# Which engine normalises the third tile of the next block's input: GpSimd or ScalarE

## The reference

```
n = layernorm(x)
s = sigmoid(silu(n @ s_w1.T + s_b1) @ s_w2.T + s_b2)
u = (n @ B_w.T + B_b) * s
h[t] = h[t-1] @ A.T + u[t]                       # a scan over 4096 steps, state of 128
x1 = x + (h @ C_w.T + C_b + n @ D_w.T + D_b) * sigmoid(n @ g_w.T + g_b)
m = layernorm(x1)
e = argmax(m @ gate_w.T)                         # one of 8 experts for each row
out = x1 + (m + m @ expert_w[e].T)
```

## Time and profile before

| what | value |
| --- | --- |
| median of three runs | 909.34 us (908.67 to 910.84) |
| the profiled execution | 911.03 us, span of the core 909.2 us |
| TensorE busy | 890.7 us, 98% |
| VectorE busy | 684.2 us, 75% |
| ScalarE busy | 635.5 us, 70% |
| GpSimd busy | 426.8 us, 47% |
| blocks | from 15.1 us to about 675 us |
| granted TensorE clock | 0.998 of full |

### The profile page before, as it was taken

One profiled execution on the slowest core, in us unless ns is written; L12 is line 12 of the kernel. 1 busy time (PEld: TensorE's weight loads), 2 busy tenths in 40 slices (PEclk: granted clock), 3 DMA queues, 4 the chain that ended last, 5 costly groups with the idle time before them and its releaser, 6 DMA issues. The chain is left out here.

```text
span 909.2 us, 15716 instructions
## 1 busy us (share of the span) xinstructions
PE 890.7 (98%) x4413; PEld 719.8 (79%) x4414; DVE 684.2 (75%) x1697; ACT 635.5 (70%) x880; POOL 426.8 (47%) x671
## 2 busy tenths in 40 slices
PE   8999999999999999999999999999999999999996
PEld 7778878787887878787787878787878887888884
DVE  6778888888887888888887888888686465555552
ACT  5568697978879687977879687978634445666661
POOL 1134537282735537282836546282624453433442
PEclk9999999999999999999999999999999999999999
DMA  9436495867758486867768495856989979998871
GB/s 319 131 93 148 93 213 140 200 144 193 157 155 209 101 213 137 201 145 189 148 169 206 95 221 128 202 145 161 293 285 401 370 239 252 216 226 220 196 184 49
DMA packets 231050, 172.37 MB, mean 190 GB/s; under 512 B 155701, under 2 KB 189237, under 8 KB 229952
## 3 DMA queue, kind: packets, MB, share of 16 engines
q1 hardware_dynamic: 220032, 137.71, 60.8%
q0 software_dynamic: 10800, 33.70, 11.3%
q10 hardware_dynamic: 144, 0.07, 0.0%
HBM read 81.63 MB, written 54.68 MB: 150 GB/s over the span
## 5 line engine op out<-in xcount | busy, mean ns | idle before, releaser
L1798 PE MATMUL y<-experts,x1T_hi 128*128 x568 | 180.5, 399 | 0.7 <-DVE x1T_lo L1422 0.7
L666 POOL DMA_INDIRECT out<-gate,ids x71 | 72.6, 1023 | 110.3 <-DVE gate L1441 69.0
L602 POOL TENSOR_SCALAR ln_var_eps<-ln_mean_var 128x4 f32<-128x4 f32 x16 | 3.7, 231 | 252.6 <-DVE ln_mean_var L1097 252.5
L1798 PEld LDWEIGHTS y<-experts,x1T_hi 128*128 128x128 f32 x568 | 103.2, 188 | 20.6 <-issue 0.9
L1798 PE MATMUL y<-experts,x1T_lo 128*128 x284 | 111.4, 392 | 0.0
L1476 PE MATMUL gates<-GwT_hi,xT_hi 128*128 128x512 f32 x256 | 105.0, 410 | 1.6
L592 POOL TENSOR_TENSOR y_biased<-y_biased,gate 128x256 f32<-128x256 f32 x120 | 94.1, 805 | 23.8 <-DVE y_biased L1087 23.6
L1476 PE MATMUL y<-DwT_hi,xT_hi 128*128 128x512 f32 x256 | 102.6, 401 | 0.0
L1441 DVE TENSOR_TENSOR gate<-y,raw_weights 128x512 f32<-128x512 f32 x71 | 49.1, 691 | 69.2 <-PE y L1798 65.1
L1478 PE MATMUL gates<-GwT_hi,xT_lo 128*128 128x512 f32 x256 | 100.6, 393 | 0.0
L1477 PE MATMUL gates<-GwT_lo,xT_hi 128*128 128x512 f32 x256 | 100.6, 393 | 0.0
(11 more groups left out here) (285 smaller groups left out, 2335.1 us busy)
## 6 DMA issues: line engine op xcount, KB each, us to landing
raw_weights<-routed_rows SPq DMA_DIRECT2D x71, 258.0 KB, 3.2
x_in<-L_attn_x SPq DMA_DIRECT2D x32, 512.0 KB, 4.5
x_rows<-L_attn_x SPq DMA_DIRECT2D x32, 512.0 KB, 4.9
turned_experts<-raw_weights SPq DMA_DIRECT2D x32, 512.0 KB, 3.5
experts<-turned_experts SPq DMA_DIRECT2D x8, 2048.0 KB, 14.7
raw_weights<-L_ffn_expert_w SPq DMA_DIRECT2D x32, 256.0 KB, 3.1
routed_rows<-padrow SPq DMA_DIRECT2D x9, 258.0 KB
out<-gate,ids POOLq DMA_INDIRECT x71, 4.1
```

The source lines that it names most:

```text
L666: nc.gpsimd.indirect_dma_start(out=out_rows, out_offset=bass.IndirectOffsetOnAxis(ap=ids[r][:, 0:1], axis=0), in_=res[r], in_offset=None, ...
L1798: ins = nc.tensor.matmul(Y[m % 2][:], x2T[a][:, k, m % 2 * P:(m % 2 + 1) * P], flat[:, bass.ds(first + (w * KD + k) * D, D)], start=(k == ...
```

## The change

In every block but the last, the third tile (i = 2) of the next block's input is normalised by ScalarE in `halve(b+1,2)`, ahead of its halves, as the first two tiles are; GpSimd normalises the fourth tile only. `xn_ready` now counts three of ScalarE's tiles a block and `xn_late` one of GpSimd's, and the waits on them follow. The work itself is the same: a tile of 128 x 512 in float32, times `rs1`, plus `shift1`.

```diff
@@ rstd1 of GpSimd @@
                 if b > 0:
-                    pool.wait_ge(S_["xn_ready"], NT + NT // 2 * (b - 1))
-                    wait(pool, S_["xn_late"], NT // 2 * (b - 1))
+                    pool.wait_ge(S_["xn_ready"], NT + (NT - 1) * (b - 1))
+                    wait(pool, S_["xn_late"], b - 1)
@@ body of GpSimd @@
                 if b < LASTB:
-                    normalise_late(b + 1, 2)
                     normalise_late(b + 1, 3)
@@ halve of ScalarE @@
-                if i < NT // 2:
+                if i < NT - 1:
                     normalise1(b, i)
-                    act.wait_ge(S_["xn_ready"], NT + NT // 2 * (b - 1) + i + 1)
+                    act.wait_ge(S_["xn_ready"], NT + (NT - 1) * (b - 1) + i + 1)
                 else:
-                    act.wait_ge(S_["xn_late"], NT // 2 * (b - 2) + i + 1)
+                    act.wait_ge(S_["xn_late"], b)
```

## The result

The first comparison gave 904.55 us (median of four runs, 904.29 to 905.12) against 909.11 for the kernel before: 4.6 us less, a ratio of 0.9947 with an interval of 0.993 to 0.9964. Two more comparisons on chips of their own gave 0.9946 (0.9933 to 0.996) and 0.9945 (0.9931 to 0.9958). The forecast was 904.8.

A forecast was written before the change was run, and what follows sets the result against it. TensorE, 98% busy, bounds the kernel, waiting on VectorE instructions that GpSimd's normalisations hold. Terms: 4.3 (twelve blocks) + 0.4 (block 0) - 0.1 (block 1) = 4.6 off 909.34, giving 904.7, stated as 904.8; range 902.8 to 908.6.

The forecast's parts named there:

- What bounds the kernel and where TensorE waits: Blocks 3 to 14: TensorE loses 0.21 at level 2's scan product and 0.27 before gates(b,1), behind VectorE instructions GpSimd holds.
- The subtraction from 0.65 to 0.29: VectorE's subtraction after the cast, no longer held by GpSimd's second normalisation, gains 0.36 a block, 4.3 us over twelve.
- The cast: VectorE's cast of the scan's ends stays held by the first normalisation until 328.42 in block 7, near 0.68 us.
- no other gap of over 0.05: Apart from those two waits, TensorE has no larger gap in blocks 3 to 14, except 0.40 where block 10 starts.
- Block 0: Its subtraction is held too, 0.78 instead of 0.29; freeing TensorE's scan product gains up to 0.49, taken as 0.4.
- Block 1: No ScalarE wait between its last two halves, so the fourth tile's transpose goes 0.84 later; 0.1 lost.
- Block 2: The cast goes free and the subtraction is held by the first normalisation, which stays: gain 0.
- ScalarE hidden: ScalarE's added 0.84 a block disappears in its 1.46 wait at the second scoresT, leaving 0.26.
- A: No gain: the subtraction is slow for another reason, or VectorE then waits for something else; some 909.2 us, chance 0.13.
- B: Slower: the fourth tile's transpose meets the third's or comes late, 0.40 lost in 13 blocks; 909.9, chance 0.07.
- D: Part: only the scan product's 0.21 a block is gained, gates(b,1) still waiting; 906.8 us, chance 0.13.
- C: More: TensorE's remaining wait before gates(b,1) goes too; 903.3 us, or 901.1 with all restarts, chance 0.07.

The follow-up runs named there:

- e2b_same_kind: Changed kernel plus a second GpSimd instruction on a spare tile, its scalars taken from rs1 and shift1 like a normalisation; 911.44 us, ratio 1.0007.
- e9_wait_between: Kernel before, both normalisations on GpSimd, with a wait between them for the subtraction of the scan's second over step; 903.36 us, ratio 0.9925.
- e2_both: Changed kernel plus a second GpSimd instruction on a spare tile, with two constants as factors; 907.83 us, ratio 0.9979.
- e10_wait_ahead: Kernel before, both normalisations on GpSimd, with the wait for the scan's subtraction ahead of both; 902.66 us, ratio 0.9927.
- e1_third: Changed kernel, unedited, measured again in the third group against the kernel before; 904.50 us, ratio 0.9945.
- e3_no_third: Changed kernel, but nobody normalises the third tile of blocks 1 to 15; 903.19 us, ratio 0.9932.
- e8_scalar_twice: Changed kernel plus one more ScalarE instruction of 0.8 us on a spare tile, ahead of the third tile's normalisation; 908.27 us, ratio 0.997.
- e5_all_on_scalar: Changed kernel, but ScalarE normalises all four tiles and GpSimd none; 909.88 us, ratio 1.0002.
- e6_gap: Kernel before, with GpSimd clearing a spare tile of 128x256 between its two normalisations; 914.84 us, ratio 1.0042.

## Why the prediction was right

**What bounds the kernel and where TensorE waits: right.** Both of the waits of the earlier trace rows went when the second normalisation left GpSimd, came back with `e2b_same_kind`, and went again in `e9_wait_between`, with GpSimd's work unchanged. That is the shown cause.

**The subtraction from 0.65 to 0.29: right. The cast: mis-sized.** The step read "the cast is still held until 328.42". The cast had been held by the second normalisation too, for 0.18 more: it went from 0.68 to 0.50, was 0.49 beside the shorter stand-in of `e2_both` and was 0.66 in `e2b_same_kind`. What in the second instruction adds the 0.18 (its operands or its length) was not separated. With both terms VectorE is ready 0.54 earlier, and TensorE loses no 0.21 ahead of the scan product, 0.10 less between its halves and 0.23 of the 0.27 ahead of `gates(b,1)`. A typical block gained 0.53 where the sum had 0.36. In the first trace blocks 3 to 14 took 486.1 us instead of 492.4: 6.3 less, instead of 4.3. Block 9 gained 0.82, since the late transpose of before came less late, and block 10 only 0.21: there GpSimd came 0.7 later than in the blocks beside it and held the subtraction (0.74). The prediction's remark that a block has no other gap of over 0.05 isn't right: block 7 has steps of 0.28 to 0.32, where 0.23 is usual, at five more places. Four of them are in the trace of `e10_wait_ahead` too, in which nothing is held.

**Block 0: 0.9 instead of 0.4, with luck in it.** The scan product's wait is gone, worth 0.48. The rest is a wait of TensorE in the preparation (0.32 in the trace of before), which stands in some traces and not in others. The block's start moves as well: with its 0.79 the first trace was only 0.10 ahead at the end of block 0. Three traces of the changed kernel have 43.40, 42.93 and 43.36 for that block.

**Block 1: 0 instead of 0.1.** It took 41.51 as before; the fourth tile's transpose landed sooner than in the trace of before, which hid its later issue.

**Block 2: 0.64 lost instead of 0.** This is the step that failed: in block 2 "the cast goes free and the subtraction is held by the first normalisation, which stays: 0". It took GpSimd's time in the block as given. In the changed kernel VectorE's last `xT_lo` of block 1 started 0.03 behind GpSimd's power instruction, which was held (1.61 instead of 1.05). GpSimd then came 0.6 later in block 2, and held the short addition ahead of the scan (0.27) and the cast of level 2 (0.35).

The fourteen traces divide cleanly. In six the `xT_lo` starts 0.02 to 0.03 behind the power instruction, which takes 1.60 to 1.61, and block 2 takes 41.26 to 41.84. In eight it starts 0.07 to 0.30 behind, the power instruction takes 1.04 to 1.05, and block 2 takes 40.42 to 40.94. All six have ScalarE's added instruction in block 1; of the seven traces that have it only `e1_third` is among the eight. What sets the 0.03 is `xT_hi` of the fourth tile, for which `xT_lo` waits: it ends 0.12 to 0.37 ahead of the power instruction's start in the six and 0.04 to 0.26 behind it in the eight. So ScalarE's added work made `xT_hi` earlier there, not later, since the fourth tile's transpose, issued later, took less time: from the end of the halves to ScalarE's join 3.8 to 4.5 us in the seven traces with that work, 5.3 to 5.4 in the seven without it. Why it takes less, and in `e1_third` (4.5) not enough less, is not shown.

**ScalarE hidden: right, with less to spare than said.** The sum left 0.26 of the wait; with 0.53 instead of 0.36 it leaves 1.46 - 0.84 - 0.53 = 0.09, and the trace shows none. `e3_no_third` shows that the 0.84 costs nothing in blocks 3 to 14, `e8_scalar_twice` that the next 0.8 costs some 2 us, and `e5_all_on_scalar` that 0.84 behind the wait costs the whole gain.

**The total.** The two terms of other sign, more in blocks 3 to 14 and less in block 2, partly cancel. The traces differ by 6.2 us in the span: 6.3 from blocks 3 to 14 and 0.9 from block 0, less 0.6 in block 2 and 0.8 by block 0's later start, and 0.4 behind the last block's start. The medians differ by 4.6: the profiled execution of before was 1.9 above its median, that of after 0.6 above. So part of the close hit is luck.

**The rivals.** A fell with the blocks' length. B did not come: `flipped` was late for a moment in single blocks, as before. D fell, as TensorE's second wait went with the first. C, more than the forecast, was the truth for blocks 3 to 14 and not for the whole. The Trainium skill's SBUF page (Who interferes with whom), by which the loser is blocked whole, fits the cast in `e6_gap`, which ended 0.25 behind the clearing instruction for an own length of 0.23. Elsewhere the rows fit less well. The subtraction ends 0.13 to 0.14 behind the second normalisation also in `e2b_same_kind` (330.28 against 330.14 in block 7), less than its own 0.29, and the cast of the changed kernel ends 0.09 behind the normalisation. Whether part of a held instruction runs ahead, or GpSimd's reported end is late, no run separates; the sum goes by the measured ends.

## What to carry to other kernels

An engine with half its time free can still set the pace, if its instructions come beside another engine's on the path; compare the durations of one form within a block, since a blocked instruction shows as a long one and not as idle time. Before moving such work to another engine, try to move it in time: one wait on a semaphore gave at least the same gain here, and left ScalarE its 0.9 us of cover a block. And a cover used up to 0.1 us is a debt: `e8_scalar_twice` lost some 2 us by the next 0.8. Moved work also changes the order elsewhere: look, where a block differs from the others (here block 1), for the pairs of engines that now start together. A difference of under 0.1 us between two starts decided over 0.6 in the next block.

## What the runs showed of the hardware

- A clearing instruction of GpSimd, which reads nothing, held VectorE's cast until its end: 0.94 instead of 0.47 to 0.52, ending 0.25 behind it. The Trainium skill's SBUF page (Who interferes with whom) says that a cast in a 2-port mode, one that uses VectorE's second pair of ports, which is GpSimd's too, and a GpSimd instruction exclude each other, and that whoever issues first gets the pair for its whole instruction. The run agrees on the exclusion; on the order it doesn't, by the profile's starts, in which the cast (329.07) stands ahead of the clearing instruction (329.46).
- VectorE holds GpSimd as well: a power instruction on 128 x 4 took 1.61 instead of 1.05 beside a subtraction of 128 x 512 with both operands in SBUF that started 0.02 to 0.03 behind it (six traces). Where the subtraction started 0.07 to 0.30 behind it, neither was held: 1.04 to 1.05 and 0.69 (eight traces), though most of one lay inside the other. So the two did not exclude each other for the whole instruction there.
- `tensor_scalar` on 128 x 512 took GpSimd 0.61 with two constants and 0.76 to 0.81 with two columns of another tile in their place.
- VectorE's operations with one operand in PSUM (lines 1050, 1052 and 1080 as numbered before) were not held: beside the pair of normalisations in `e10_wait_ahead` they took 0.28 to 0.30 and 0.68 to 0.69, in blocks 2 to 14.
